# Two more heads of each sample take their probabilities' transpose through the DMA engines

## The reference, cut to what matters

```python
B, S, HID = (4, 128, 512)
D, HQ, HK = (128, 32, 8)
PAGES, PSIZE, NPP = (64, 32, 16)
...
bsz, seqlen, _ = x.shape
q = jnp.einsum('bsd,ed->bse', x, Wq).reshape(bsz, seqlen, HQ, D)
k = jnp.einsum('bsd,ed->bse', x, Wk).reshape(bsz, seqlen, HK, D)
v = jnp.einsum('bsd,ed->bse', x, Wv).reshape(bsz, seqlen, HK, D)
q = _rope(_rmsnorm(q, q_norm_w), pos)
k = _rope(_rmsnorm(k, k_norm_w), pos)
L = NPP * PSIZE
k_all = jnp.concatenate([k_cache[block_table].reshape(bsz, L, HK, D), k], axis=1)
v_all = jnp.concatenate([v_cache[block_table].reshape(bsz, L, HK, D), v], axis=1)
k_all = jnp.repeat(k_all, HQ // HK, axis=2)
v_all = jnp.repeat(v_all, HQ // HK, axis=2)
scores = jnp.einsum('bqhd,bkhd->bhqk', q, k_all) * SCALE
scores = jnp.where(valid[:, None, None, :], scores, -1e+30)
probs = jax.nn.softmax(scores, axis=-1)
o = jnp.einsum('bhqk,bkhd->bqhd', probs, v_all).reshape(bsz, seqlen, HQ * D)
return jnp.einsum('bse,de->bsd', o, Wo)
```

## Time and profile before

| | |
|---|---|
| median of 3 runs | 1301.6 us (1301.73, 1301.6, 1297.05) |
| the profiled execution | 1296.74 us |
| its span | 1295.1 us |
| one unit in the loop | 31.1 us |

### The profile page before, as it was taken

One profiled execution on the slowest core, in us unless ns is written; L12 is line 12 of the kernel. 1 busy time (PEld: TensorE's weight loads), 2 busy tenths in 40 slices (PEclk: granted clock), 3 DMA queues, 4 the chain that ended last, 5 costly groups with the idle time before them and its releaser, 6 DMA issues.

```text
span 1295.1 us, 26067 instructions
## 1 busy us (share of the span) xinstructions
PE 1277.9 (99%) x6698; PEld 1092.6 (84%) x6698; DVE 935.0 (72%) x2658; ACT 784.7 (61%) x1834; POOL 768.0 (59%) x792
## 2 busy tenths in 40 slices
PE   9999999999999999999999999999999999999998
PEld 8888877887888888888888888888888888888886
DVE  6532457778777777877777788777777977777774
ACT  6731334556666668676666676766656767656664
POOL 2110011348766668787666697866667869666663
PEclk9999999999999999999999999999999999999999
DMA  8321224176655558756555677655556775555543
GB/s 295 103 82 49 73 71 142 55 268 193 130 126 131 129 124 214 185 125 142 129 130 126 133 205 190 126 131 135 132 132 160 185 186 132 125 124 124 124 96 82
DMA packets 314896, 179.57 MB, mean 139 GB/s; under 512 B 260418, under 2 KB 279234, under 8 KB 314562
## 3 DMA queue, kind: packets, MB, share of 16 engines
q1 hardware_dynamic: 295840, 125.83, 40.8%
q0 software_dynamic: 12032, 35.40, 10.4%
q10 hardware_dynamic: 6946, 17.44, 4.4%
HBM read 119.71 MB, written 16.91 MB: 105 GB/s over the span
## 4 chain that ended last, share of the span: by engine, by line
PE 78%; SPq 7%; issue 5%; DVE 4%; POOL 2%; DMA 2%; ACT 1%; POOLq 0%; DVEq 0%; ACTq 0%
PE bank L1624 15%; PE tail L1662 13%; PE wide L1692 12%; PE tail L1729 10%; PE wide L464 4%; PE wide L1656 4%; PE wide L544 3%; PE bank L1645 3%; PE bank L464 3%; PE tail L464 3%; SPq L1513 2%; SPq L1527 2%; PE wide L599 2%; SPq L1552 2%; DMA turned<-parts 1%
## 5 line engine op out<-in xcount | busy, mean ns | idle before, releaser
L1662 PE MATMUL tail<-prT,vt 128*128 128x512 f32 x960 | 258.5, 409 | 0.7 <-POOL prT L1410 0.5
L1662 PEld LDWEIGHTS tail<-prT,vt 128*128 128x128 f32 x960 | 172.0, 190 | 40.4 <-DVE prT L2077 10.0
L1343 POOL TENSOR_TENSOR tick<-tick 128x1 f32<-128x1 f32 x254 | 57.9, 228 | 220.7 <-PE tail L1662 77.0
L1729 PE MATMUL tail<-woT,oT 128*128 128x512 f32 x768 | 179.5, 389 | 0.9 <-DVE oT L2129 0.9
L1729 PEld LDWEIGHTS tail<-woT,oT 128*128 128x128 f32 x768 | 144.0, 188 | 31.2 <-DVE oT L2129 1.3
L1692 PE MATMUL wide<-kT,qT 128*128 128x320 f32 x512 | 158.7, 310 | 1.8 <-DVE mx L2105 1.5
L1692 PE MATMUL wide<-kT_low,qT 128*128 128x320 f32 x512 | 158.2, 309 | 0.0
L1692 PE MATMUL wide<-kT,qT_low 128*128 128x320 f32 x512 | 157.9, 308 | 0.0
L1401 POOL TENSOR_TENSOR parts<-raw,parts 128x1280 f16<-128x1280 f32 x55 | 145.7, 2648 | 8.0
L1874 ACT ACTIVATE raw<-raw,nm,q_scale 128x640 f32<-128x640 f32 x124 | 114.6, 924 | 46.6 <-DVE nm L2108 45.0
L1874 ACT ACTIVATE pr<-pr,nm,q_scale 128x640 f32<-128x640 f32 x128 | 117.9, 921 | 35.7 <-DVE nm L2108 34.9
(11 more groups left out here) (289 smaller groups left out, 2852.4 us busy)
## 6 DMA issues: line engine op xcount, KB each, us to landing
w_ring<-pair_weights SPq DMA_DIRECT2D x80, 256.0 KB, 3.9
k_raw<-k_pages SPq DMA_DIRECT2D x512, 32.0 KB, 1.7
v_raw<-v_pages SPq DMA_DIRECT2D x512, 32.0 KB, 2.8
spread<-one_over_denominators ACTq DMA_DIRECT2D x32, 512.0 KB, 4.8
xTb<-x_transposed POOLq DMA_DIRECT2D x31, 512.0 KB, 4.1
rope<-rope_tables SPq DMA_DIRECT2D x31, 256.0 KB, 2.7
out<-y POOLq DMA_DIRECT2D x31, 256.0 KB, 5.4
...
```

The costliest lines, as they stand in the source:

```text
L1343: nc.gpsimd.tensor_tensor(tick[:, 2:3], tick[:, 1:2], tick[:, 1:2], ALU.add).then_inc(s_carry, 1)
L1662: last = nc.tensor.matmul(tail[g][:, :], vt[v_part][:, j, g * D:(g + 1) * D], prT[p_part][:, :, j, :], start=(j == v_part == p_part == 0), ...
L1729: last = nc.tensor.matmul(place[:, :], oT[:, g, o_part, (h % REP) * S:(h % REP + 1) * S], woT[w_part][:, h, :], start=(h == o_part == w_pa ...
```

## The change

Units of samples 2 to 5 of each pair, 16 of 32, get a "third" couple of heads through the DMA engines: heads 4 and 5, the first half of the second group. Their exponentials lie side by side in `pr_third`. POOL halves them (`halve_third`) into `parts[0]` after the first couple's tiles there have been turned, SP turns the two tiles (`turn_third`) into `turned_third`, which lies over `pr_third`; ACT casts the first part to `prT[0]` (`high_turned_third`), POOL the rest to `prT[1]` (`low_turned_third`), both in the next turn. TensorE leaves out the transposes of these heads; ACT's and DVE's copies out of PSUM take two heads in place of four.

The order changes with it in the turns that have such a back (3 to 6). On TensorE the key transposes come ahead of the first group's lows, these stand together ahead of the second wide tile, and the second group's ten highs come before its five lows. DVE makes both of its low parts in a row, after the first group's lows. SP loads the rope table first, puts the four transposes among the last five key loads, and the two new ones after 4 of the 16 value loads. `spread` moves to the space of `parts[1]`, so its load waits for the last of the four first transposes, in every turn. Turns 2 and 6 now stand outside the hardware loop.

```diff
-    pr = [place(135168 + h * 2560 if h < 6 else 163840 + (h - 6) * 2560, f"pr{h}", [P, NK]) for h in range(REP, HP)]
+    pr_third = place(145408, "pr_third", [P, HALF, NK])
+    pr = [pr_third[:, h, :] for h in range(HALF)] + [place(163840 + h * 2560, f"pr{REP + HALF + h}", [P, NK]) for h in range(HALF)]
...
-    spread = place(135168, "spread", [P, G, REP * S])
+    turned_third = [place(145408 + i * 2560, f"turned_third{i}", [P, HALF * JT, S], F16)[:, :, :] for i in range(2)]
+    spread = place(140288, "spread", [P, G, REP * S])
...
+    THIRDS = range(2, 6)
+
+    def has_third(b):
+
+        return b in THIRDS if isinstance(b, int) else True
+
+    def thirds(pair, b):
+
+        done = min(max(b - THIRDS[0], 0), len(THIRDS)) if isinstance(b, int) else b - THIRDS[0]
+        return done + pair * len(THIRDS)
...
-            with eng.Fori(0, B - 3) as last:
-                turn(pair, last + 2, before(last + (pair * B + 2)), True, True, True, None, True, True)
+            turn(pair, 2, before(pair * B + 2), True, True, True, None, True, True)
+            with eng.Fori(0, len(THIRDS) - 1) as last:
+                turn(pair, last + 3, before(last + (pair * B + 3)), True, True, True, None, True, True)
+            turn(pair, 6, before(pair * B + 6), True, True, True, None, True, True)
...
+        def halve_third(u, before, n):
+
+            pool.wait_ge(s_exp, u * HP + 3 * HALF)
+            for i in range(2):
+                pool.wait_ge(s_turned[0][i], (u + before) * 16 + 16)
+            carry(n)
+            nc.gpsimd.tensor_copy(parts[0][:, 0], pr_third[:, :, :]).then_inc(s_half, 1)
+            pool.wait_ge(s_half, u * 2 + before + 3)
+            nc.gpsimd.tensor_tensor(parts[0][:, 1], pr_third[:, :, :], parts[0][:, 0], ALU.subtract).then_inc(s_rest[0], HALF)
+
+        def low_turned_third(u, before, n):
+
+            pool.wait_ge(s_turned[0][1], (u + before) * 16 + 32)
+            pool.wait_ge(s_pv, u * G + 1 + FIRST)
+            carry(n)
+            nc.gpsimd.tensor_copy(prT[1][:, 0:HALF].rearrange("p h j q -> p (h j) q"), turned_third[1]).then_inc(s_tl, 1)
+
...
                 split_keys(u, n)
+                n = n + 1
+            if has_third(b - 1):
+                low_turned_third(u - 1, thirds(pair, b - 1), n)
                 n = n + 1
...
+        def turn_third(pair, b):
+
+            u, before = unit(pair, b), thirds(pair, b)
+            sp.wait_ge(s_rest[0], (u + before) * HALF + 2 * HALF)
+            for i in range(2):
+                sp.sem_inc(s_seen, 1)
+                sp.dma_start_transpose(turned_third[i], parts[0][:, i].rearrange("p h n -> p (h n)")).then_inc(s_turned[0][i], 16)
...
+            if has_third(b - 1):
+                load_rope(pair, b)
+                load_keys(pair, b, pages, 0, KEYS_FIRST)
+                turn_part(pair, b - 1, 0, 0)
+                load_keys(pair, b, pages, KEYS_FIRST, KEYS_FIRST + 2)
+                turn_part(pair, b - 1, 0, 1)
+                load_keys(pair, b, pages, KEYS_FIRST + 2, KEYS_FIRST + 4)
+                turn_part(pair, b - 1, 1, 0)
+                load_keys(pair, b, pages, KEYS_FIRST + 4)
+                turn_part(pair, b - 1, 1, 1)
+                load_values(pair, b, pages, 0, VALUES_FIRST)
+                turn_third(pair, b - 1)
+                load_values(pair, b, pages, VALUES_FIRST)
...
+        VALUES_FIRST = 4
...
+                if third:
+                    pe.wait_ge(s_rope, n * G + 2 + FIRST)
+                    transposes(0, [ra[:, REP + i, :] for i in range(G)])
+                    probs_wide(1, 0)
+                    sums(0, range(JT), (0,), 1).then_inc(s_pv, 1)
+                    probs_wide(1, 1)
+                elif front:
...
+                if not third:
+                    pe.wait_ge(s_rope, n * G + 2 + FIRST)
+                    transposes(0, [ra[:, REP + i, :] for i in range(G)])
+            if back and front and not third:
...
-            if back:
+            if third:
+                pe.wait_ge(s_yadd, u + FIRST)
+                pe.wait_ge(s_th[0], u + before_back + 2)
+                for w in range(2):
+                    pe.wait_ge(s_phi, u * 3 + w + 1)
+                    sums(1, (2 * w, 2 * w + 1), (0, 1), 0)
+                pe.wait_ge(s_phi, u * 3 + 3)
+                sums(1, (JT - 1,), (0, 1), 0)
+                for w in range(2):
+                    pe.wait_ge(t_free[w], u + 1 + FIRST)
+                pe.wait_ge(s_tl, u * 2 + before_back + 3)
+                sums(1, range(JT - 1), (0,), 1)
+                begin(0)
+                sums(1, (JT - 1,), (0,), 1).then_inc(s_pv, 1)
+            elif back:
...
-                ac.copy(prT[0][:, :, 2 * w:2 * w + 2, :].rearrange("p h j q -> p j h q"),
-                        wide[w][:, :].rearrange("p (j h q) -> p j h q", j=2, h=REP)).then_inc(s_phi, 1)
...
+                ac.copy(prT[0][:, first_head:, 2 * w:2 * w + 2, :].rearrange("p h j q -> p j h q"),
+                        wide[w][:, 0:2 * heads_there * S].rearrange("p (j h q) -> p j h q", j=2, h=heads_there)).then_inc(s_phi, 1)
+
+            def high_turned_third():
+
+                act.wait_ge(s_turned[0][0], (u + before_back) * 16 + 32)
+                ac.copy(prT[0][:, 0:HALF].rearrange("p h j q -> p (h j) q"), turned_third[0]).then_inc(s_th[0], 1)
...
-                act.wait_ge(s_turned[0][1], u * 16 + 16)
+                act.wait_ge(s_turned[1][1], u * 16 + 16)
...
                 high(0, 3, kT[:, :, L:NK], bank[0][:, 0:G * S].rearrange("p (g c) -> p g c", g=G))
+            if third:
+                high_turned_third()
             if back:
                 high_probs(0)
+            if third:
+                high_probs(1)
             if front:
             if back:
-                high_probs(1)
+                if not third:
+                    high_probs(1)
...
+                if not front or third:
                     dve.wait_ge(s_pv, u * G + 1 + FIRST)
...
                 low_probs(0)
+            if third:
+                low_probs(1)
```

180 lines of the change are left out of this document (103 added, 77 removed).

## The result

| | before | after |
|---|---|---|
| median | 1300.75 us (4 runs, 1297.05 to 1301.73) | **1317.6 us** (4 runs, 1312.34 to 1325.32) |
| the profiled execution | 1296.74 us, span 1295.1 | 1315.85 us, span 1314.0 |

The ratio is 1.014, 95% interval 1.0083 to 1.0196. I had forecast 1283.5 and a range up to 1300. The change makes the kernel slower by some 17 us, where I expected 18 us off.

A forecast was written before the change was run, and what follows sets the result against it. TensorE, busy 99% of the span, was taken as the bound. 20.5 us gained less 2.4 charged gives 18.1 off 1296.74, so 1278.6; the median lies 4.9 higher: 1283.5 us, range 1275 to 1300.

The forecast's parts named there:

- TensorE's part of the sum: On TensorE, ten transposes less in each of 16 units plus the new order: 1.28 us a unit, 20.5 us off.
- T to S: From the next turn's first transposes to the end of that unit's sums, where scores start: 9.2 us forecast, 10.33 before.
- T - S: From the end of a unit's sums to the next turn's first transposes: still 20.75 us.
- The order's 0.18 us a unit: TensorE's sums: highs first removes the wait for DVE (0.15 us), and fewer transpose-matmul changes; 0.18 us a unit gained.
- The first place on POOL: POOL's chain from the scores' start to the next first transposes: third `halve` fits, cost zero, slack 0.3 to 0.4 us.
- The old wait of 2.29 us: POOL's wait for a DMA transpose; with 0.35 us of slack it pays for the third `halve`'s 4.13 us.
- The charge of 0.15 us a unit for the fifth cast: Inside the sums, TensorE's second-group lows wait for POOL's cast after `split_keys`; no slack, 0.15 us a unit, 2.4 in all.
- Other turns: zero: Turns without a third couple: `spread` waits for a later tile that TensorE awaits anyway; cost zero.
- the paragraph on SP and the DMA engines: SP's queue and DMA: new tiles issued by 653.5, landed by 655.6, value loads with 0.8 us of slack; cost zero.
- DMA lands late; slower: Rival: first couple's second tile and 12 value loads land late, 1.45 us a unit, 23 us, 1325 us; chance 0.13.
- The rival of POOL: POOL sets the period: third `halve` 0.9 us dearer, transposes and lows late; only 7 us off, 1294.6 us; chance 0.22.

The follow-up runs named there:

- e5: The change with the third couple's two tiles moved by plain DMA copies of the same 320 KB in place of DMA transposes: 1282.1 us.
- e1: The change's order on TensorE, ACT and DVE only, all four heads of the second group transposed on TensorE, no third couple: 1292.64 us.
- e15: The change with x, `spread` and y cut to 16 of 128 partitions and 12 value loads to 4 of 32 rows, in third-couple turns: 1281.36 us.
- e11: The change with POOL issuing the load of x between the two operations of `split_keys` in turns with a third back: 1292.76 us.

## Why the prediction was wrong, by its own steps

**What held.** TensorE's part of the sum stands. 160 transposes less gave what they should: with e5 as witness T to S is 9.17 us (I had 9.2), T - S 20.76 (20.75), the unit 29.9 (29.9). The order's 0.18 us a unit was 0.2 by e1's units (31.1 to 30.9); its whole, 6.8 us, came out above my 16 x 0.18 = 2.9, and TensorE's wait for POOL at T is a part of the rest (the earlier trace rows had 6.7 us, e1 3.5). The first place on POOL, "cost zero, slack 0.3 to 0.4", is right to the tenth: in e5 the last cast ends at 679.92 + 1.25 = 681.17, and T is 681.53. The old wait of 2.29 us did pay for the third `halve`. The charge of 0.15 us a unit for the fifth cast is not seen where its tile is in time; e5's fifteen matmuls run through in 3.53 us. In sum e5's 16 units take 478.34 us and those of the kernel before 497.35: 19.0 less, where I had 18.1. What did not hold is "Other turns: zero": the other 14 units behind 307 us take 449.3 us in e5 and 444.3 before. That is one execution of each, and the runs of the kernel before lie 5 us apart themselves, so how much of it is the change is open.

**The step that failed** is the paragraph on SP and the DMA engines: "its tiles are issued by 653.5 and land by 655.6", and at its end "Cost zero, but the loads now share the DMA engines, busy 55%, with `spread`, x and the y store". I took 3.5 us from the earlier trace rows, the landing of the first couples' transposes. Those fly between T - 14 and T - 2, ahead of the large loads. The new ones are issued from T - 2 on, and x and `spread` are issued at T - 0.2. I named these three transfers and did not put their issue times beside the new transposes'. Instead of 3.5 us the tiles took up to 13.3, where POOL wanted them at T + 6.2. The 0.55 of the earlier trace rows is a unit's mean; over the 8 us that counted it was 0.63 already, and 1.21 after the change. The value loads went the same way: 4.3 us in the median for the 2.8 of the earlier trace rows, 0.8 us of slack, and POOL waits for them in half the units, 27.0 us in all. The size: the 16 units of the change take 513.6 us, 35.3 more than in e5. Of these 25.9 lie between T and S, where TensorE stands for the fifth cast, and 9.4 between S and the next T, where POOL's chain starts with the wait for `v_raw`.

**The rival** "DMA lands late; slower" (1325, chance 0.13) is the case that happened in kind, and that its size is near (1317.6) is luck. It put all of the loss between S and the next T, where 9.4 of the 35.3 us are. Its second half was right, 12 value loads late. Its first half had the wrong tile: I put the delay on the first couple's second tile, awaited by `halve_third`, whose landing stayed at 3.4 in the median and 5.8 at most. It is the *new* tiles that land late, and the wait sits in the fifth cast, in the place that I had listed under POOL and priced at 0.15 us a unit. Measured against e5 the collision costs 1317.6 - 1282.1 = 35.5 us, 2.2 us for each of the 16 units. My evidence against it, "the median transpose is near the shortest", came from transposes issued at another place in the unit, ahead of the large loads, so it said nothing on this.

**Not in any case of mine** was the clock. A stall of 6 us was followed by matmuls at half speed, 2.1 us more in that unit.

**The rival of POOL** gets no support where it was placed: POOL works as long in e5 and e15 as in the change, and their units with a third couple keep 29.8 to 29.9 us but for a few. TensorE still waits for POOL before the transposes at T, 9.8 us in e5 and 10.4 in e15, for the most part in the other units (e1 had 3.5).

**What stays open.** How the delay goes in detail on the DMA engines (turns, packets, or something in the transposes' writes) was not measured, only that few packets or few neighbours end it. Nor is it shown how much of e5's gain is the shorter issue. And no order was found in which the full transfers give 1282, or less than the order alone gives (e1, 1292.64). The best is e11 with 1292.76. Of the 9.5 us that its 16 units have over e5, 5.4 lie between T and S, since POOL's issue of x now stands ahead of the fifth cast, and 4.2 between S and T, where POOL waits for values, 36.1 us in all.
